# A one-hot that compares with a constant in PSUM instead of a scalar in SBUF: one line of a graph network's first edge pass

## The reference, cut to what matters

```
h = relu(layernorm(x));  deg = segment_sum(w, src)
w_norm = dinv[src] * w * dinv[dst]
x = x + relu(segment_sum(w_norm[:, None] * (h @ kernel)[dst], src) + bias)
h = relu(layernorm(x))
messages over both directions: concat(h[end], edge_attr) @ W + b, summed per node,
divided by the count, leaky relu, + h, layernorm, added to x
```

## Time and profile before

| what | us |
|---|---|
| median of three runs (4246.0 to 4250.3) | 4246.62 |
| the profiled execution, its own time | 4252.24 |
| its span in the trace | 4250.4 |
| PE busy | 3448.3 |
| DVE busy | 3101.1 |
| POOL busy | 3055.5 |
| ACT busy | 1865.2 |
| POOL, scatters of `first_layer` (L827), 864 | 1439.4 |
| DVE, `spread_hot` (L870), 108 | 126.2 |

### The profile page before, as it was taken

The page is one execution under the profiler, slowest core; times in us unless marked ns, Lnnn a source line. Parts: engine busy times, 40 slices in busy tenths (PEclk is TensorE's granted clock), DMA queues, the critical chain, the costliest instruction groups (busy, mean ns, idle before and its releaser), DMA issues. The chain is left out here.

```text
span 4250.4 us, 99711 instructions
## 1 busy us (share of the span) xinstructions
PE 3448.3 (81%) x30414; PEld 2895.6 (68%) x30630; DVE 3101.1 (73%) x7790; ACT 1865.2 (44%) x4527; POOL 3055.5 (72%) x1813
## 2 busy tenths in 40 slices
PE   3455699888889889889834789898989898898987
PEld 3344687777777777777724677777777677777666
DVE  8799888888888888888726766666766676666423
ACT  1020455555555555555424344444444444444523
POOL 4778688888888888888841888777877787787210
PEclk8788899999999999999966799999999999999965
DMA  9992787777777777777777555444544455454931
GB/s 174 272 234 16 157 144 143 139 136 141 136 143 143 134 142 138 136 145 135 141 145 204 82 84 81 79 78 80 85 79 78 78 80 81 77 83 70 132 100 31
DMA packets 731785, 505.05 MB, mean 119 GB/s; under 512 B 306293, under 2 KB 643226, under 8 KB 731236
## 3 DMA queue, kind: packets, MB, share of 16 engines
q0 software_dynamic: 257584, 176.81, 37.0%
q1 hardware_dynamic: 473528, 321.32, 29.1%
q10 hardware_dynamic: 124, 0.05, 0.0%
HBM read 284.18 MB, written 240.17 MB: 123 GB/s over the span
## 5 line engine op out<-in xcount | busy, mean ns | idle before, releaser
L827 POOL DMA_INDIRECT gcn_sums<-fl_sums,fl_to_i x864 | 1439.4, 1666 | 293.6 <-DMA gcn_sums<-fl_sums,fl_to_i 155.0
L1686 POOL DMA_INDIRECT gcn_sums<-shared,ds_to_i x752 | 1293.9, 1721 | 466.4 <-ACT shared L1937 245.1
L1892 PE MATMUL bank<-ds_counts,ds_parts 128*128 128x256 bf16 x3675 | 606.8, 278 | 0.0
L1961 ACT COPY ds_turned<-bank 128x1024 bf16<-128x1024 bf16 (+1 forms) x325 | 313.2, 964 | 598.4 <-PE bank L1877 467.9
L1055 ACT COPY fl_sums<-bank 128x256 f32<-128x256 f32 x864 | 325.3, 377 | 552.7 <-PE bank L983 342.2
L1925 ACT CAST ds_counts<-bank 128x392 bf16<-128x392 f32 x800 | 382.6, 491 | 219.9 <-PE bank L1836 191.9
L865 DVE SCALAR_TENSOR_TENSOR fl_same<-fl_key_b,fl_pat,bank 128x128 f32<-128x128 bf16 x864 | 372.7, 443 | 113.9 <-PE bank L983 91.1
L1912 PE MATMUL bank<-ds_turned,ds_now 128*128 128x512 bf16 (+1 forms) x1734 | 420.7, 372 | 12.1 <-issue 0.9
L1854 PE MATMUL bank<-shared 128*128 128x128 f32 x1504 | 310.4, 311 | 118.3 <-DVE attr_sums L1738 89.7
L1821 DVE TENSOR_TENSOR src_sums<-src_sums,bank 128x512 f32<-128x512 f32 (+1 forms) x325 | 212.9, 655 | 261.7 <-PE bank L1912 257.4
L982 PE MATMUL bank<-fl_pay,fl_same 128*128 128x128 f32 x1728 | 348.5, 284 | 48.9 <-issue 34.7
(11 more groups left out here) (264 smaller groups left out, 7167.6 us busy)
## 6 DMA issues: line engine op xcount, KB each, us to landing
fl_attrs<-in_edge_attr SPq DMA_DIRECT2D x108, 512.0 KB
shared<-in_edge_attr SPq DMA_DIRECT2D x186, 256.0 KB
fl_rel_b<-dst_offset SPq DMA_DIRECT2D x108, 256.0 KB
fl_key_b<-src_key SPq DMA_DIRECT2D x108, 256.0 KB
gcn_sums<-zeros SPq DMA_DIRECT2D x40, 640.0 KB
shared<-src_key SPq DMA_DIRECT2D x94, 256.0 KB
gcn_sums<-fl_sums,fl_to_i POOLq DMA_INDIRECT x864
near<-src_float SPq DMA_DIRECT2D x1, 12892.0 KB
```

The lines of the kernel that those rows point to most:

```text
L827: nc.gpsimd.indirect_dma_start(out=d.tab_gcn[j % K], out_offset=bass.IndirectOffsetOnAxis(ap=to_i[:, (GPI * kk + gi) % 4, j:j + 1], axis=0 ...
L1686: nc.gpsimd.indirect_dma_start(out=d.tab_gcn[j % K].rearrange("n (two f) -> (n two) f", two=2), out_offset=bass.IndirectOffsetOnAxis(ap=to ...
L1892: ins = nc.tensor.matmul(row_bank[:, 0:2 * P], parts[:, tile, s, :], counts[:, h, tile, :, :].rearrange("p b q -> p (b q)"), start=(tile = ...
```

## The change

The partition number is also kept in the PSUM bank of constants, in 8 columns behind the two constants there, and L870 becomes an instruction with two tensor inputs: `rel_b` from SBUF as before, and those columns from PSUM, column j repeated 128 times. The copy into PSUM is one more instruction at the start of the stage, and the wait behind the constants counts it. Result, size and types of `spread_hot` stay, and so do all semaphores of the loop. On every engine the instructions stand in the order of before; only the form of L870 is another (in the changed kernel it is L871, and the lines behind it are one or two further on).

```diff
         iota_c, from_me_c = (const_bank[:, k * P:(k + 1) * P] for k in range(2))
+        part_c = const_bank[:, 2 * P:2 * P + J]
...
                 if j == 2:
                     dve.wait_ge(rel_in[h], 16 * loads(i, kk, gi))
                     at_least(dve, row_ready, 2 * g)
-                    nc.vector.tensor_scalar(spread_hot[:], rel_b[:, h, :, :].rearrange("p q j -> p j q"), d.part[:, 0:1], None,
+                    nc.vector.tensor_tensor(spread_hot[:], rel_b[:, h, :, :].rearrange("p q j -> p j q"), part_c.unsqueeze(2).to_broadcast([P, J, P]),
                                             ALU.is_equal).then_inc(spread_ready, 1)
...
             nc.vector.tensor_copy(from_me_c, d.from_me[:]).then_inc(const_ready, 1)
+            nc.vector.tensor_copy(part_c, d.part[:]).then_inc(const_ready, 1)
             nc.vector.tensor_copy(numbers[:], d.iota[:]).then_inc(const_ready, 1)
-            dve.wait_ge(const_ready, 3)
+            dve.wait_ge(const_ready, 4)
```

## The result

The changed kernel takes 4280.37 us (median of four runs, 4279.13 to 4281.41) where the kernel before takes 4246.31 beside it: a ratio of 1.0083, interval 1.0065 to 1.0100. It is 34 us **slower**; the forecast was 4213, a gain of 34, with a range that ended at 4248. The profiled execution took 4281.41 us, its span 4279.6, 29.2 more than before.

The account below looks back on a forecast made before the run. POOL was taken as the stage's bound, 64.1 us a slot against 61.4 for PE and DVE. Afterwards PE and DVE bound at 62.9, ending the stage at 2146.6 instead of 2180.8: 34 us gained, 4213, range 4187 to 4248.

Parts of the forecast that it names:

- The instruction at 2.0 us: DVE's two-input compare replacing L870: 2.0 us instead of 1.17, +0.83 us a group, +90 us of DVE's busy time.
- both estimates from rows: New compare's length: 1.95 us from L841 plus the stepping cost of L865 over L1409; 2.06 from L870 itself.
- The hold of L870 on POOL: Scatters beside L870 take 0.64 us longer on average; gone with the PSUM operand, 2.6 us a slot.
- The change of sides: Stage's bound moves from POOL, then at 61.5 us a slot, to PE and DVE at 62.9.
- The waits that became longer: PE's L1014 waits for DVE's L904: 0.83 us longer at a slot's start, new in the other groups.
- the 1.57 of the sum: Growth of a slot by PE and DVE: 0.83 + 0.1 + 0.32 + 0.32 us, from 61.37 to 62.9.
- the full buffer of sums: PE's 3.53 us standstill, in the slot behind the one of 61.37 us, read as waiting for room there.
- 61.4 us a slot: Own pace claimed for PE and DVE before the change, taken from one slot, against POOL's 64.1.
- the 58 us of POOL: Scatter time saved over 108 instructions, chosen from 44 to 69 us; POOL falls from 64.1 to 61.5 us a slot.
- The dear instruction: Rival, 12%: DVE's new compare takes 2.55 us, adding 3.8 us a slot: 24 us slower, 4271.
- The hold stays: Rival, 8%: the two-input form keeps POOL waiting just as long, nothing won or lost: 4247.
- cheap: Rival, 12%: stepping costs DVE's two-input compare nothing (1.22 us), POOL's pace decides, 58 us won: 4189.

Follow-up runs that it names:

- experiment 5: Changed kernel with six more 128x128 matmuls on PE ahead of its wait for the weighed one-hots in each slot's last group: 4269.73 us.

## Why the prediction was wrong

**Right.** The instruction at 2.0 us (2.03, and (2.03 - 0.14) / 1024 = 1.85 ns an element; both estimates from rows, 1.95 and 2.06, were near). The Trainium skill, "Vector Engine (DVE) Microarchitecture Reference", section 5.2, gives 1.73 ns an element where one source hops 4 KiB at every element; the trace comes near it, with steps of 16 bytes. The hold of L870 on POOL (0.57 us each; I had 0.64) and its end with the PSUM operand. The change of sides. The waits that became longer: in slots with a jump the period went from 66.5 to 68.2 us, +1.7 against the 1.57 of the sum. The copy into PSUM cost nothing seen: the first L871 starts at 449.2, where it was 449.6.

**The step that failed** is "PE stands still for 3.53 us with no event, which I read as waiting for room in the full buffer of sums", and so "PE and DVE by themselves need 61.4 us a slot". It was the jump, and their pace was 64.0. The row said "issue", and I gave it a cause that fitted; the loop's own line names the right one. Corrected, with nothing else touched: ten of the 22 slots take 66.5 instead of 61.37, +51 us, and 4213 becomes 4264, which is slower than before.

**A term left out**: the clock. A longer pause was costed as its length. In slots without a jump it also brought the lower clock, and the period rose from 61.4 to 64.0, 2.6 us where 1.57 was in the sum; about 1.0 for each of the 12 such slots is 12 us (experiment 5 gave back 1.0 in each of them, 5 to 11 us in all). 4264 + 12 = 4276, against 4280.37, and the same working puts the end of the stage at 2210, against 2208.9. The sum is this close with estimates of 1 us a slot in it, so a part of the closeness is luck.

**A term too large**: the 58 us of POOL. With the three loops written out the stage ended 23 us sooner by the free POOL (2175.8 to 2152.7), and 28 us sooner than before (2180.7), whatever the instruction took. POOL needed 62.7 us a slot there (1.618 + 0.341 for each scatter), where the prediction had 61.5. The size of this term did not decide the result.

**The rivals.** The dear instruction would have given 4271, the nearest time of the forecast's and the rivals', by a mechanism that did not happen (it needed 2.35 us). "The hold stays" and "cheap" are both excluded by rows. None of them had the true cause, since all took the 61.4 for granted: so the range was too narrow for a reason that more rivals of the same kind could not have mended.

## What to carry to other kernels

Before an idle "issue" gets a cause, look up the loop's own line: a jump back cost PE and DVE 4 to 5 us each here. Taking out PE's alone won nothing, and taking out PE's, DVE's and ACT's together did; DVE's alone wasn't tried. When two sides of a pipeline are compared, take the pace of each over whole passes of the loop and not over the best slot, since an edit that frees the one by loading the other pays only as far as the other has real slack. And a PE pause that grows from 1.8 to 2.9 us can cost more than 1.1 us: here it brought the half clock with it in most slots, and products put into the pause won time.

## What was new about the chip

- A hardware loop's jump took 3.8 to 4.2 us on PE's sequencer, 4.3 to 5.3 us to the next instruction on DVE's and 2.7 to 3.4 on ACT's, but 0.3 on POOL's, in the same loop of before.
- Idle for 1.25 or 1.83 us, PE kept its full clock at the places shown; behind 2.87 us it was at 0.50 for over 3 us. The length of a pause alone doesn't decide it: in the changed kernel 15 of the 19 such pauses between 690 and 1890 us (2.5 to 2.9 us) had a stretch at 0.50 right behind them, and with the three loops written out none of the first ten (2.5 to 2.7 us, to 1250 us) had one.
- A comparison of 1,024 elements read in steps of 16 bytes takes 2.03 us with two inputs (in order: 1.22) and 1.17 with one (in order: 0.75), and whether the second input lies in SBUF or PSUM changes nothing in it (2.03 both, stepped).
- That place decides POOL's wait: 1.05 us of each instruction with both in SBUF, 0.01 with one in PSUM, 0.57 for the single-input form.
